# Routed experts: f32 products in place of three f16 products, and the one-hot tiles' product with the shares on GpSimd

## What is computed

```python
def _L0_ffn_ref(inputs, gamma, beta, w_q, keys, key_in, key_out):
    ...                                   # feature norm over all tokens -> xn
    q = (xn @ w_q.T).reshape(b, n, 2, h, kd).transpose(2, 0, 1, 3, 4)
    sim = jnp.einsum('pbnhd,hkpd->pbnhk', q, keys)      # 2 x 8 heads x 64 keys
    s, i = jax.lax.top_k(sim, k)                        # 8 best of each side
    ...
    scores, pk = jax.lax.top_k(all_scores, k)           # 8 best pairs
    idx = jnp.take_along_axis(all_idx, pk, axis=-1)     # of 4096 experts
    w_down = key_in[idx]
    w_up = key_out[idx]
    o = jnp.einsum('bnd,bnhkd->bnhk', inputs, w_down)
    o = jax.nn.gelu(o, approximate=False) * jax.nn.softmax(scores, axis=-1)
    return jnp.einsum('bnhk,bnhkd->bnd', o, w_up)
x = x + _L0_attn_a_ref(_layernorm(x), ...)
x = x + _L0_ffn_ref(_layernorm(x), ...)
x = x + _L0_attn_b_ref(_layernorm(x), ...)
x = x + _L0_ffn_ref(_layernorm(x), ...)
```

## Time and profile before

| | |
|---|---|
| time, median of 3 runs | 3398.86 us (3397.81 to 3402.24) |
| the profiled execution, its own time | 3402.41 us |
| its span, from the first to the last instruction | 3400.6 us |
| mean granted TensorE clock | 0.975 of full speed |
| first routed stage, first score product to last residual | 318.6 to 1299 us |
| second routed stage | 2416.9 to 3397 us |

### The profile page before, as it was taken

One profiled execution on the slowest core, in us unless ns is written; L12 is line 12 of the kernel. 1 busy time (PEld: TensorE's weight loads), 2 busy tenths in 40 slices (PEclk: granted clock), 3 DMA queues, 4 the chain that ended last, 5 costly groups with the idle time before them and its releaser, 6 DMA issues. The chain is left out here.

```text
span 3400.6 us, 74937 instructions
## 1 busy us (share of the span) xinstructions
PE 3180.5 (94%) x29442; PEld 2235.4 (66%) x29442; DVE 2876.6 (85%) x8980; ACT 1644.9 (48%) x2256; POOL 677.0 (20%) x357
## 2 busy tenths in 40 slices
PE   8998799999999988799999999998789999999997
PEld 7886588888888867333333333334568888888886
DVE  5757899999999996788888888882799999999996
ACT  4534444444444434346556656565344444444441
POOL 0000233333333340200000000000033333333333
PEclk9998999999999999799999999998899999999999
DMA  4225000000000005631212111003300000000000
GB/s 154 80 60 161 10 15 11 20 11 20 11 20 11 17 8 167 166 64 34 37 33 51 34 34 36 8 6 113 102 8 11 20 11 20 11 20 11 20 8 17
DMA packets 130869, 140.56 MB, mean 41 GB/s; under 512 B 29974, under 2 KB 115926, under 8 KB 130518
## 3 DMA queue, kind: packets, MB, share of 16 engines
q1 hardware_dynamic: 120918, 126.72, 14.1%
q10 hardware_dynamic: 9600, 9.05, 0.9%
HBM read 84.75 MB, written 50.59 MB: 40 GB/s over the span
## 5 line engine op out<-in xcount | busy, mean ns | idle before, releaser
L490 PE MATMUL f_p_route<-f_x_w,f_y_hot 128*128 128x64 f16 x8192 | 902.4, 194 | 54.1 <-DVE f_weighted L768 42.9
L514 PE MATMUL f_p_out<-kout_in,f_hidden 128*128 128x256 f16 x6144 | 853.7, 273 | 17.5 <-POOL f_hidden L408 16.5
L503 PE MATMUL f_p_hid<-f_xtc,kin_in 128*128 128x256 f16 x6144 | 856.0, 274 | 5.9 <-ACT f_hidden L604 5.8
L408 POOL TENSOR_TENSOR f_hidden<-f_weighted,f_hidden 128x1024 f16<-128x1024 f32 x256 | 612.5, 2393 | 1217.4 <-DVE f_x_w L758 1213.2
L2066 DVE TENSOR_REDUCE at_part_max<-at_p_ring 128x1 f32<-128x512 f32 (+3 forms) x1280 | 706.1, 603 | 113.0 <-PE at_p_ring L1945 74.8
L490 PEld LDWEIGHTS f_p_route<-f_x_w,f_y_hot 128*128 128x128 f16 x8192 | 697.2, 98 | 96.2 <-issue 60.9
L514 PEld LDWEIGHTS f_p_out<-kout_in,f_hidden 128*128 128x128 f16 x6144 | 600.0, 98 | 196.0 <-issue 118.6
L503 PEld LDWEIGHTS f_p_hid<-f_xtc,kin_in 128*128 128x128 f16 x6144 | 602.4, 98 | 80.0 <-issue 10.1
L609 ACT CAST f_hidden<-f_weighted 128x1024 f16<-128x1024 f32 x256 | 342.9, 1340 | 465.3 <-DVE f_weighted L768 465.3
L604 ACT ACTIVATE f_hidden<-f_p_hid 128x512 f32<-128x512 f32 x512 | 301.9, 596 | 500.5 <-PE f_p_hid L503 497.3
L1945 PE MATMUL at_p_ring<-at_k,at_q 96*128 96x512 bf16 (+3 forms) x1280 | 416.3, 362 | 40.0 <-DVE at_m_rest L2083 15.4
(11 more groups left out here) (272 smaller groups left out, 3451.1 us busy)
## 6 DMA issues: line engine op xcount, KB each, us to landing
at_q<-qk SPq DMA_DIRECT2D x42, 256.0 KB, 4.5
at_k<-qk SPq DMA_DIRECT2D x42, 256.0 KB, 4.3
x<-f_ln_y SPq DMA_DIRECT2D x32, 256.0 KB, 2.8
xt<-f_ln_xt SPq DMA_DIRECT2D x32, 256.0 KB, 3.6
f_xt_in<-xt SPq DMA_DIRECT2D x32, 256.0 KB, 2.8
f_xres<-x SPq DMA_DIRECT2D x32, 256.0 KB, 2.7
qk<-ap_parts_q SPq DMA_DIRECT2D x16, 384.0 KB, 3.8
qk<-ap_parts_k SPq DMA_DIRECT2D x16, 384.0 KB, 5.0
```

The lines of the kernel that those rows point to most:

```text
L408: nc.gpsimd.tensor_tensor(lo, weighted[s % WR], hi, ALU.subtract).then_inc(lo_ready, 1)
L490: last = nc.tensor.matmul(p_route[:, t, :], y_hot[:, s % HR, t // PAIR, :, t % PAIR], x_w[:, s % HR, half, t // PAIR, :, t % PAIR], start= ...
L503: last = nc.tensor.matmul(p_hid[g % 2][:, xp % 2, :], kin_t[:, a, dh, xp * P:(xp + 1) * P], xt[slot][:, b, dh, :], start=i % 6 == 0, stop= ...
L514: last = nc.tensor.matmul(p_out[:, u, :], parts[slot][:, xp, u * P:(u + 1) * P, a], kout[:, b, xp, :], start=g == 0 and i == 0, stop=xp == ...
```

## The change

Expert products are made in f32 from unsplit operands: `hidden`, `xt`, `kin_in`, `kout_in` are f32 tiles, a group has 4 products instead of 12, and all splitting is gone: ScalarE's lines 574 and 609, GpSimd's 400 and 408, and in `memory_gradients` ScalarE's rounding of `key_out` and VectorE's lines 1239 and 1275. `weigh` writes `hidden` in place, and `expert_out` waits for `routed` (the weighing) and no longer for the low parts. The input tile becomes a ring of three (`XR`). `x_w` moves from VectorE to GpSimd in all eight steps (`GP_STEPS`), `hot` becomes a ring of two, and a semaphore `tiles_shared` tells TensorE that `x_w` is made; VectorE's next `hot` on the same slot waits for it too. The key scores and the routing products stay as they were.

```diff
-HR, WR = 2, 2
+HR, XR = 2, 3
+GP_STEPS = tuple(range(NS))
...
-        xt = [sb(f"xtc{b}", [P, 2, DH, CH], F16) for b in range(2)]
+        xt = [xt_in] + [sb(f"xtc{b}", [P, DH, CH]) for b in range(XR - 1)]
...
-        hot = sb("hot", [P, PS // PAIR, 2 * NX, PAIR], F16)
+        hot = sb("hot", [P, HR, PS // PAIR, 2 * NX, PAIR], F16)
...
+            def share_tiles(c, slot, s):
+                pool.wait_ge(p_lo_ready, ONE + c + 1)
+                pool.wait_ge(hot_steps, ONE + c * NS + s + 1)
+                above(pool, route_ready, c * NS + s + 1 - HR)
+                nc.gpsimd.tensor_tensor(x_w[:, s % HR, :, :, :, :], hot[:, s % HR, :, :, :].unsqueeze(1).to_broadcast(BOTH),
+                                        shares_of(slot, s), ALU.mult).then_inc(tiles_shared, 1)
+
+            for c in range(NCH):
+                for s in GP_STEPS:
+                    share_tiles(c, c % 2, s)
...
                     pe.wait_ge(hot_ready, ONE + c * NS + s + 1)
+                    if s in GP_STEPS:
+                        pe.wait_ge(tiles_shared, ONE + gp_steps_below(c * NS + s + 1))
...
-            EXPERT_STEPS = 12
+            EXPERT_STEPS = 4
...
-                last = nc.tensor.matmul(p_hid[g % 2][:, xp % 2, :], kin_t[:, a, dh, xp * P:(xp + 1) * P], xt[slot][:, b, dh, :],
-                                        start=i % 6 == 0, stop=i % 6 == 5)
+                xp, dh = 2 * g + i // DH, i % DH
+                last = nc.tensor.matmul(p_hid[g % 2][:, xp % 2, :], kin_t[:, dh, xp * P:(xp + 1) * P], xt[c % XR][:, dh, :],
+                                        start=dh == 0, stop=dh == DH - 1)
...
             def expert_out(c, slot, g, i):
                 if i == 0 and g == 0:
-                    pe.wait_ge(lo_ready, ONE + c * NS + NS)
+                    pe.wait_ge(routed, ONE + c * NS + NS)
...
+                last = nc.tensor.matmul(p_out[:, u, :], hidden[slot][:, xp, u * P:(u + 1) * P], kout[:, xp, :],
...
-                            for i in range(j % PS * 3 // 4, (j % PS + 1) * 3 // 4):
+                            for i in range(j % PS // 4, (j % PS + 1) // 4):
...
-                nc.vector.tensor_tensor(weighted[s % WR], h, p_route[:].rearrange("p t (u x) -> p x u t", u=2),
+                nc.vector.tensor_tensor(h, h, p_route[:].rearrange("p t (u x) -> p x u t", u=2),
...
-            ("wct_in", [P, DH, NSUB], F32), ("kin_in", [P, 2, DH, NE], F16), ("kout_in", [P, 2, NX, D], F16))]
+            ("wct_in", [P, DH, NSUB], F32), ("kin_in", [P, DH, NE], F32), ("kout_in", [P, NX, D], F32))]
```

More of the change, by code:

```diff
@@ L303, in pb @@
             return ctx.enter_context(nc.psum_tensor(tag + name, shape, F32))
-        parts = [h[:].rearrange("p x t -> p (x t)").bitcast(F16).rearrange("p (x t k) -> p x t k", x=NX, k=2) for h in hidden]
-        xt = [sb(f"xtc{b}", [P, 2, DH, CH], F16) for b in range(2)]
+        xt = [xt_in] + [sb(f"xtc{b}", [P, DH, CH]) for b in range(XR - 1)]
         xn = sb("xn", [P, DH, CH])
@@ L329, in routed_experts @@
         y_hot = sb("y_hot", [P, HR, PS // PAIR, P, PAIR], F16)
-        hot = sb("hot", [P, PS // PAIR, 2 * NX, PAIR], F16)
+        hot = sb("hot", [P, HR, PS // PAIR, 2 * NX, PAIR], F16)
         x_w = sb("x_w", [P, HR, 2, PS // PAIR, 2 * NX, PAIR], F16)
-        ring = [sb(f"weighted{i}", [P, NX * 2 * PS]) for i in range(WR)]
-        weighted = [r[:].rearrange("p (x u t) -> p x u t", x=NX, u=2) for r in ring]
         xres = sb("xres", [P, 2, D])
@@ L383, in exists, with gp_steps_below @@
             return not isinstance(c, int) or 0 <= c < NCH
+        def gp_steps_below(k):
+            return len([i for i in range(k) if i % NS in GP_STEPS])
         block = ctx.enter_context(nc.Block())
@@ L420, in _ @@
                     nc.gpsimd.memset(ahead.up[n], 0.0).then_inc(ahead.up_zero, 1)
-            rounds(pool, one)
+            def share_tiles(c, slot, s):
[7 more added lines that the diff above has]
+                    share_tiles(c, c % 2, s)
         x_view = x_dram.rearrange("(n p) d -> p n d", p=P)
@@ L750, in one_hots @@
                 above(dve, hot_ready, c * NS + s)
-                nc.vector.tensor_tensor(hot[:], y_iota[:, 0:2 * NX, :].unsqueeze(1).to_broadcast(wide), tokens(xq[slot], wide),
+                if s in GP_STEPS:
+                    above(dve, tiles_shared, gp_steps_below(c * NS + s + 1 - HR))
+                nc.vector.tensor_tensor(hot[:, s % HR, :, :, :], y_iota[:, 0:2 * NX, :].unsqueeze(1).to_broadcast(wide), tokens(xq[slot], wide),
                                         ALU.is_equal).then_inc(hot_steps, 1)
-                nc.vector.tensor_tensor(y_hot[:, s % HR, :, :, :], y_iota[:].unsqueeze(1).to_broadcast(tall), tokens(yq[slot], tall),
-                                        ALU.is_equal)
-                dve.wait_ge(hot_steps, ONE + c * NS + s + 1)
-                if s == 0:
-                    dve.wait_ge(p_lo_ready, ONE + c + 1)
-                nc.vector.tensor_tensor(x_w[:, s % HR, :, :, :, :], hot[:].unsqueeze(1).to_broadcast(both),
-                                        shares[slot][:, s, :, :].rearrange("p h (t k) -> p h t k", k=PAIR).unsqueeze(3).to_broadcast(both),
-                                        ALU.mult).then_inc(hot_ready, 1)
+                last = nc.vector.tensor_tensor(y_hot[:, s % HR, :, :, :], y_iota[:].unsqueeze(1).to_broadcast(tall), tokens(yq[slot], tall),
+                                               ALU.is_equal)
+                if s not in GP_STEPS:
+                    dve.wait_ge(hot_steps, ONE + c * NS + s + 1)
+                    if s == 0:
+                        dve.wait_ge(p_lo_ready, ONE + c + 1)
+                    last = nc.vector.tensor_tensor(x_w[:, s % HR, :, :, :, :], hot[:, s % HR, :, :, :].unsqueeze(1).to_broadcast(BOTH),
+                                                   shares_of(slot, s), ALU.mult)
+                last.then_inc(hot_ready, 1)
             def weigh(c, slot, s):
```

111 lines of the change are left out of this document (30 added, 81 removed).

## The result

The changed kernel takes 3896.7 us in the median of 4 runs (3892.6 to 3897.3), the one before took 3398.9 in 4 runs beside it (3397.8 to 3402.2). The ratio is 1.146, 95% interval 1.144 to 1.148. The prediction was 3924 us, range 3785 to 3990. The profiled execution has a span of 3895.3 us against 3400.6 before, 494.7 more.

A forecast was written before the change was run, and what follows sets the result against it. TensorE was taken to bound the rounds. Start, rounds and tail add 262.6 us a routed stage, of which rounds 1 to 13 hold 224; two stages add 525 to 3398.9, giving 3924 us, range 3785 to 3990.

The forecast's parts named there:

- The product of f32: On TensorE, one f32 expert product takes 0.4315 us and replaces three f16 products of 0.327 together: +1.67 us a step.
- The weight load behind a routing product: On TensorE, each of eight spread expert products pays 0.08 us of unhidden weight load: +0.64 us a step.
- rival 1: No load stall on TensorE: a step of 8.72 us, a round of 70.1, time 3791 us; chance 0.10.
- Loads overlap: On TensorE, f32 weight loads overlap the running product, with 256-column passes 0.216 us apart.
- Rival 4: On TensorE, f32 loads don't overlap with products: 680 us more, time 4600 us; chance 0.01.
- rival 3: Not slower: the number of weight loads sets TensorE's pace, passes under 0.17 us, time 3290 us; chance 0.03.
- Rounds 1 to 13 don't wait for GpSimd: GpSimd's product stays hidden in the middle rounds: tiles need 12.6 us, TensorE's stretches give 14.2.
- Rival 2: GpSimd becomes the bound from about 5.5 us a product: 4175 us at 7, about 4550 at 9.6; chance 0.13.
- GpSimd's product: GpSimd's new product of one-hot tiles and shares takes 4.8 us, with ends of 3.5 and 9.6.
- The prediction's walk to 62: Round 0, with VectorE, GpSimd and TensorE in a deciding chain, goes from 57.55 to 62 us: +4.8, bounds 52 and 70.
- Start, round 14 and tail: Stage ends: +6.7 us before the first `hot`, +2.5 to the first weighing, round 14 +10.8, tail +2.9.
- The exclusion: VectorE's operations with two SBUF inputs and GpSimd's work exclude each other; otherwise rounds 0 and 15 cost 45 us less.

The follow-up runs named there:

- Experiments 2 and 3: Changed kernel with spread expert products in pairs behind eight routing products, then fours behind sixteen: 3817.7 us, then 3785.1 us.
- Experiment 7: Changed kernel with each 256-column expert_in product issued as four of 64 columns, values not the layer's: 4804.2 us, measured once.
- experiment 4: Changed kernel with VectorE making `y_hot` ahead of `hot`: 3900.7 us, ratio 1.148 to the kernel before.
- experiment 1: Changed kernel with the shares' product back on VectorE in all steps, f32 products kept: 3880.8 us, ratio 1.142 to the kernel before.
- Experiment 9: Kernel before with GpSimd's rest of the hidden values (line 408) left out, shares on VectorE: 3362.3 us, ratio 0.989.
- experiment 5: Kernel before with choosing work moved between VectorE's steps, key search to step 3 and maxima to step 6: 3438.2 us, ratio 1.011.

## Why the prediction was right, and where it was off

**The product of f32: right.** A product was put at 0.4315 us from the earlier trace rows. Runs of four take 0.43 each in the changed kernel, at the same full clock.

**The weight load behind a routing product: right.** It was read from two rows, and it was the weakest reading of the large terms. The step came out at 9.38 us against 9.36. Experiments 2 and 3 take four and then two of the eight stalls away and get 0.33 and 0.16 us back; rival 1, with no stall, falls. Experiment 7 paces short f32 passes at the same 0.11 us. One figure for the load gives both numbers, though no run separates the load from another fixed cost of an f32 pass.

**Loads overlap: right.** Rival 4 needed 32 x 0.109 us more in a step, and rival 3 passes under 0.17 us apart; both fall. The Trainium skill ("TensorE: Matmul & The Clock Gate", section "The mechanism") says that loads overlap only across row groups; f32 passes with full 128x128 loads keep 0.216 us here, so the trace disagrees once more.

**Rounds 1 to 13 don't wait for GpSimd: right,** and they don't in any version with f32 products. The row of line 404 has six waits in the kernel, none of them in these rounds. Rival 2 falls.

**GpSimd's product: too large.** This is the term that was mis-sized. The prediction took 4.8 us by doubling, and set tiles and GpSimd one behind the other, 1.73 + 4.8 = 6.53 a step. Recorded are 4.47, and the record holds the waiting for `y_hot`: with no two-input work of VectorE behind its start the product has 3.61 (experiment 4), near the lower end, 3.5, which the prediction had given for f16 inputs. In round 15 a step is the recorded 4.47 and the 0.68 between one product and the next, 5.15 together. Round 15 thereby costs 1.2 us and not 10.7. Round 0 gains 1.9 and doesn't lose 4.8, but there the product's size is only a part of it: with no product on GpSimd at all it still takes 54.7 us (experiment 1), and with fewer stalls 51.4 to 53.9 (experiments 2 and 3). The prediction's walk to 62 let the chain over GpSimd decide every step; TensorE waited visibly for GpSimd in two. How much of the 6.7 us is the product's size is not shown. The two rounds were 16.2 us a stage too high, the whole sum 15.3; the other five parts differ by 1 to 1.9 each and nearly cancel. That the time came within 0.7% of the forecast is owed to the middle rounds, which are nine tenths of the sum.

**Start, round 14 and tail: small, with things missing.** Ahead of the first `hot` the prediction took 20.9 us for the products of chunk 0 before, where the earlier trace rows have 21.7 (329.12 to 350.86); the new ones also start 0.7 us earlier (328.42), so +5.2 and not +6.7. Behind the first `hot` it had the routing at its old 3.7 us, of which 3.3 had been at the lower clock already. With f32 products in it and the lower clock for nearly all of it, it took 6.0, which the shorter GpSimd product partly made good (11.4 against 10.4 predicted). Round 14 is 1.7 us shorter than predicted, since its last step has no run of `expert_in` any more (6.54 us against 8.52 in the steps before). In the tail the products begin 2.6 us behind the last weighing (1515.08 to 1517.72) and not 1.2, since VectorE's residual of chunk 14 (line 752) stands ahead of them.

**The exclusion: right.** The prediction took it from one meeting. The changed kernel shows it at both stages' start (3.98 us for a `hot` of 0.68) and at every `hot` of round 15; experiment 4 shows it in GpSimd's record. The Trainium skill ("SBUF — State Buffer", section "Who interferes with whom") says the same, as the prediction told; the runs here add that the waiting engine's record grows, whichever of the two waits. One sign was wrong: GpSimd's record doesn't begin when `y_hot` ends, but 0.2 us behind its start, and holds the wait.

**What VectorE's longest steps cost the kernel before: incomplete.** The prediction said that 1.3 us a round is all that relief of VectorE can give back. Experiment 9 relieves VectorE of most of GpSimd's interference and gets 0.4 us a round; experiment 5 moves work out of the long steps and loses 1.1. The steps are long partly because of GpSimd, and the order of VectorE's work behind the weighing decides how much. The forecast didn't rest on it, since TensorE covered VectorE in rounds 1 to 13 of the changed kernel. The whole price of GpSimd's rest in the kernel before is 39 us (3401.1 - 3362.3), of which rounds 1 to 13 of both stages hold 11, round 14 some 10 (51.9 us against 57.3 and 56.1) and the ends the rest. I found no version that computes everything and beats the kernel before.

## What to carry to other kernels

Price a product by its columns and passes first (three f16 products of 256 columns take 0.327 us, one in f32 0.43), and then look at what stands ahead of it: behind a product shorter than the weight load, the load is paid, so heavy loads belong in runs. Work moved to GpSimd costs by what VectorE does beside it, by what stands ahead of it in GpSimd's list, and by how soon its result is needed: add its own time, that of VectorE's held operations and the waits of the work ahead of it, and compare with the bound engine's step. A long record of an engine may hold waiting for the other one, so take its own time from where nothing runs beside it.
